# Two chained attentions on one Trainium2 core: the maxima of the softmax computed as one stream through both attentions

## The reference

```python
# layer 0, per image: group norm, then attention with relative positions, 6 heads of 16
attn = einsum('bqd,bkd->bqk', q * SCALE, k) + rel_h[..., None] + rel_w[..., None, :]
out0 = softmax(attn) @ v                       # 1024 queries x 1024 keys
x = x + out0 @ proj_w + proj_b
# layer 1, per image: layer norm, causal attention, 6 heads of 16
att = where(causal, (q @ k.T) * scale, -max)
t = t + (softmax(att) @ v) @ w_proj
# layer 1, feed-forward: 4 experts, top 2 by the gate, exact gelu
t = t + sum_e gate_e * (gelu(ln(t) @ w1_e + b1_e) @ w2_e + b2_e)
```

## The kernel before

| pair | `ahead` before |
|---|---|
| layer 1, p = 0 | 18: layer 1's own fills 6 to 23 (the first six stand ahead of the attention, `LEAD`) |
| layer 1, p = 1 | 32: own fills 24 to 47, then the first 8 of `lead` |
| layer 1, p = 2 | 24: `lead` 8 to 31 (`lead` is the maxima of pair 0 of the next image's layer 0) |
| layer 0, p = 0 | 32: `attn0` 0 to 31 |
| layer 0, p = 1 | 32: `attn0` 32 to 63 |
| layer 0, p = 2 | none |

## Time and profile before

### The profile page before, as it was taken

The page is one execution under the profiler, slowest core; times in us unless marked ns, Lnnn a source line. Parts: engine busy times, 40 slices in busy tenths (PEclk is TensorE's granted clock), DMA queues, the critical chain, the costliest instruction groups (busy, mean ns, idle before and its releaser), DMA issues.

```text
span 2026.6 us, 24544 instructions
## 1 busy us (share of the span) xinstructions
PE 1719.8 (85%) x8928; PEld 687.1 (34%) x8928; DVE 1217.0 (60%) x2498; ACT 1071.3 (53%) x1377; POOL 297.9 (15%) x191
## 2 busy tenths in 40 slices
PE   1578488998899988998899988999889989998858
PEld 0122232343333433344333433334333433234333
DVE  6743577546764577636775467646775466744631
ACT  1236435674556734665456745567445745565433
POOL 6103101401032000501023010321005010200000
PEclk7589679999999999999899999999999999999979
DMA  6645454445535346444335355353454454323000
GB/s 174 137 88 158 116 135 79 104 113 171 93 65 154 87 129 112 103 119 156 71 74 121 96 171 101 65 157 104 123 95 103 117 158 84 75 52 93 14 11 8
DMA packets 63742, 212.10 MB, mean 105 GB/s; under 512 B 17414, under 2 KB 19079, under 8 KB 51206
## 3 DMA queue, kind: packets, MB, share of 16 engines
q1 hardware_dynamic: 61702, 210.04, 42.0%
q10 hardware_dynamic: 1920, 0.49, 0.1%
HBM read 115.62 MB, written 81.79 MB: 97 GB/s over the span
## 4 chain that ended last, share of the span: by engine, by line
PE 60%; DVE 21%; ACT 7%; DMA 6%; issue 4%; SPq 2%; POOL 0%; ACTq 0%; DVEq 0%
PE psS L716 13%; DVE mx L1462 9%; PE psOM L768 9%; PE psT L746 7%; PE psT L889 5%; PE psOM L776 5%; PE psS L903 5%; PE psT L749 4%; DVE mrow L1564 3%; DVE qs L1591 2%; PE psT L666 2%; ACT probs L1143 1%; DVE x L1573 1%; DMA qs<-negr 1%; DMA qs<-scr_h 1%
## 5 line engine op out<-in xcount | busy, mean ns | idle before, releaser
L1143 ACT ACTIVATE probs<-psT 128x1024 f32<-128x1024 f32 (+7 forms) x768 | 621.4, 836 | 490.4 <-PE psT L746 240.3
L1462 DVE TENSOR_REDUCE mx<-psS 128x1 f32<-128x512 f32 (+3 forms) x1152 | 680.7, 640 | 292.2 <-PE psS L716 227.1
L746 PE MATMUL psT<-qs,ks 128*128 128x512 f32 x768 | 344.8, 522 | 38.3 <-DMA qs<-negr 17.6
L716 PE MATMUL psS<-ka,qa 128*128 128x512 bf16 x768 | 306.0, 407 | 45.2 <-DVE mx L1462 26.2
L768 PE MATMUL psOM<-probs,v 128*32 128x512 f32 x1536 | 225.5, 610 | 1.3
L716 PEld LDWEIGHTS psS<-ka,qa 128*128 128x128 bf16 x768 | 72.3, 98 | 345.4 <-DVE mx L1462 282.0
L749 PE MATMUL psT<-qr,kr 97*128 97x512 bf16 (+3 forms) x576 | 184.1, 348 | 4.6 <-DMA qr<-negb 3.7
L889 PE MATMUL psT<-xf,w1s 97*128 97x512 f32 x384 | 185.3, 616 | 1.8 <-DVE mrow L1564 1.8
L746 PEld LDWEIGHTS psT<-qs,ks 128*128 128x128 f32 x768 | 144.0, 200 | 116.7 <-ACT probs L1143 41.9
L903 PE MATMUL psS<-probs,w2s 128*96 128x512 f32 x384 | 181.5, 598 | 0.8 <-ACT att L1202 0.8
L1591 DVE TENSOR_TENSOR qs<-psOM,qs 32x768 fp32r<-32x768 f32 x128 | 121.8, 952 | 95.9 <-ACT qs L1177 93.9
(11 more groups left out here) (165 smaller groups left out, 1711.8 us busy)
## 6 DMA issues: line engine op xcount, KB each, us to landing
qs<-scr_w SPq DMA_DIRECT2D x48, 512.0 KB, 5.3
qs<-scr_q SPq DMA_DIRECT2D x48, 384.0 KB, 7.4
scr_q<-split SPq DMA_DIRECT2D x32, 384.0 KB, 4.1
scr_k<-split SPq DMA_DIRECT2D x32, 384.0 KB, 4.6
scr_w<-qs SPq DMA_DIRECT2D x8, 1536.0 KB, 12.4
scr_h<-qs SPq DMA_DIRECT2D x16, 768.0 KB, 14.7
qs<-scr_h SPq DMA_DIRECT2D x96, 128.0 KB, 5.1
qr<-scr_q SPq DMA_DIRECT2D x8, 1152.0 KB, 7.9
```

The lines of the kernel that those rows point to most:

```text
L716: last = mm(bank[:, 0:n], q[0:rows, h, t * P:(t + 1) * P], k[0:rows, h, kc * HALF:kc * HALF + n], start=True, stop=not diagonal)
L746: last = mm(o[:, a:b], ks[:, p % 2, hh, keys], qs[:, p % 2, kt // 2 % 2, hh, a:b], start=True, stop=True)
L1143: A(probs[:, n % 4, q0:T], psT[:, t_slot(ts, m), q0:T], ACT.Exp).then_inc(t_free, 1)
L1462: V.reduce_max(mx[layer][:, p % 2, (h % 2) * NT + t, kc:kc + 1], psS[:, s_bank(st, fill), 0:max_cols(layer, t, kc)], AX).then_inc(s_free, 1)
```

## The change

A function `stream(layer, p, lead, first)` now gives each pair two lists out of one sequence of fills (layer 1's own, `lead`, `attn0`): `ahead`, spread over steps 0 to 5 as before, and `tail`, of 8 fills in layer 0 and 6 in layer 1, which are the first fills of the pair behind the next. A tail's fills are issued one at a time in steps 6 and 7, in layer 0 at every call of `between`, in layer 1 at every second; what is left of it is issued after the pair's last values.

| pair | `ahead` now | `tail` now |
|---|---|---|
| layer 1, p = 0 | 18: own 6 to 23 | 6: own 24 to 29 |
| layer 1, p = 1 | 18: own 30 to 47 | 6: `lead` 0 to 5 (none for the last image) |
| layer 1, p = 2 | 26: `lead` 6 to 31 | 6: `attn0` 0 to 5 |
| layer 0, p = 0 | 26: `attn0` 6 to 31 (first image: 32, from 0) | 8: `attn0` 32 to 39 |
| layer 0, p = 1 | 24: `attn0` 40 to 63 | none |
| layer 0, p = 2 | none | none |

On VectorE `group_var` moves from 6 to 12 fills behind `group_stats`, and `group_norm` behind the last of layer 1's own fills and the `mrow` that follows it. The number of instructions of each kind on each engine stays the same.

```diff
-LEAD_EARLY = 8
+TAIL = {0: 8, 1: 6}
+
+
+def stream(layer, p, lead, first):
+
+    later = [("attn0", f) for f in range(2 * PER_PAIR[0])]
+    if layer:
+        own = [("attn1", f) for f in range(2 * PER_PAIR[1])]
+        later = own + [("lead", f) for f in range(len(MAX_STEPS["lead"]))] + later if lead else own
+    ends = [0, PER_PAIR[1], 2 * PER_PAIR[1], 2 * PER_PAIR[1] + len(MAX_STEPS["lead"])] if layer else [0, PER_PAIR[0], 2 * PER_PAIR[0], 2 * PER_PAIR[0]]
+    begin = ends[p] + TAIL[layer] if p else LEAD if layer else 0 if first else TAIL[1]
+    return later[begin:ends[p + 1]], later[ends[p + 1]:ends[p + 1] + TAIL[layer]]
...
+                    ahead, tail = stream(layer, p, next_lead(it), it is None)
+                    points, sent = [0], [0, 0]
+
+                    def issue(fills):
+
+                        for stage, fill in fills:
                             if stage == "lead" and fill == 0:
...
                             max_scores(it, stage, fill)
-                        sent[0] = until
+
+                    def between(kt):
+
+                        points[0] += 1
+                        until = min(len(ahead), len(ahead) * points[0] // (5 * (NT - 2)))
+                        issue(ahead[sent[0]:until])
+                        sent[0] = max(sent[0], until)
+                        if kt >= NT - 2 and sent[0] == len(ahead) and points[0] % (1 + layer) == 0:
+                            issue(tail[sent[1]:sent[1] + 1])
+                            sent[1] += 1
...
                     values(p, NT - 1)
+                    issue(tail[sent[1]:])
...
                     group_stats(it, "gn")
-                    maxima(it, "attn1", range(per, per + 6))
+                    maxima(it, "attn1", range(per, per + 12))
                     group_var(it, "gn")
-                    maxima(it, "attn1", range(per + 6, per + 22))
+                    maxima(it, "attn1", range(per + 12, 2 * per))
                     group_norm(it, "gn")
-                    maxima(it, "attn1", range(per + 22, 2 * per))
```

More of the change, by code:

```diff
@@ L753, in scores @@
                             last.then_inc(t_full, 1)
-                        between()
+                        between(kt)
                 def values(p, kt):
@@ L778, in values @@
                         last.then_inc(p_used, 1)
-                n = PER_PAIR[layer]
                 lead = layer == 1 and next_lead(it)
```

## The result

| | before | after |
|---|---|---|
| median of 4 runs each, us | 2025.75 (2021.58 to 2027.63) | 1997.38 (1991.79 to 2006.92) |
| ratio to before, 95% interval | | 0.9868 [0.9824, 0.9911] |
| profiled execution, us | 2028.4 | 2000.13 |

A forecast was written before the change was run, and what follows sets the result against it. VectorE, reducing through two banks, was taken to set steps 0 to 5 of the 32-fill pairs, 0.60 us per fill. The terms summed to -60.2 us from 2028.4, 1968.2, median near 1967; 8-in-10 range 1950 to 2002.

The forecast's parts named there:

- B: Layer 0, p = 0, 32 to 26 fills and a tail of 8: -8.4 us in 7 images, +1.8 in the first; -6.6.
- A: Layer 0, p = 1, 32 to 24 fills: -4.8 us a pair (ends 3.2 and 5.5), -38.4 in 8 images.
- the rule: A step with n fills lasts about (n - 1) x 0.60 + 1.29 us: 3.1, 3.7, 4.3 for 4, 5, 6.
- C: Layer 1, p = 0, a tail of 6 behind the statistics: +1.75 us in six images, +0.3 in the last two; +11.1.
- D: Layer 1, p = 1, 32 to 18 fills and a tail of 6: -5.2 us in six images, -38.9 in all.
- E: Layer 1, p = 2, 24 to 26 fills and a tail of 6: +1.8 us in seven images, +12.6 in all.
- TensorE doesn't set the steps: Rival claimed the opposite: four-fill steps no shorter than five-fill ones, gains vanish, tails cost +51 us, 2079; chance 0.06.
- The load for p = 2: Rival in layer 0's p = 1: the last load lands too late, ScalarE waits 1.6 us, 13 in all, 1980; chance 0.13.
- The clock at the ends of layer 1's pairs: Rival: new TensorE waits at two pair ends lower the clock, 12 to 20 us in all, 1984; chance 0.14.
- The opposite that it named: End of layer 1's p = 2: the tail fills the wait and lifts the clock, up to 1 us in seven images.
- What would show it: Signs expected in the profile after: the pair and step lengths, much less waiting of fills for VectorE in sum.
- three signs of being wrong: Layer 0 four-fill steps above 3.4 us, ScalarE waiting at its negation for a DMA in layer 0's p = 1, longer `mix`.

The follow-up runs named there:

- e1_join: Changed kernel with `mrow` made by a reduction over one SBUF operand instead of a two-operand maximum: 1976.6 us, 0.9735 of the kernel before.
- e8_pool: Changed kernel with the two-operand `mrow`, but GpSimd's last `den` multiplication waits until layer 0's p = 0 `mrow` is made: 1979.39 us, 0.9759 of before.
- e2_before_join: Kernel before the change, with `mrow` made by the one-operand reduction: 2030.16 us, 1.0009 of the kernel before.
- e9_meet: Kernel before, with GpSimd's last `den` multiplication delayed until the 31st reduction, so it begins just ahead of `mrow`: 2036.39 us, 1.004 of before.
- e10_meet_join: Kernel before, with GpSimd's last `den` multiplication delayed until the 31st reduction and `mrow` made by the one-operand reduction: 2028.72 us, 0.9998 of before.
- e7_step0: Changed kernel with one-operand `mrow` and four fills beside the projections in step 0 of layer 0's p = 1: 1976.55 us, 0.9742 of before.
- e5_stats: Changed kernel with one-operand `mrow` and `group_stats` six reductions earlier, among the steps of layer 1's p = 0: 1985.19 us, 0.978 of before.
- e3_no_tail0: Changed kernel without layer 0's tail (0 fills instead of 8), layer 1 as changed: 2001.47 us, 0.9857 of the kernel before.

## Why the prediction was right in direction and half in size

- **B, step 6: this failed.** "Step 6 ... now has five fills, 3.69: +0.95". It lasted 7.80 us. The working counted fills and nothing else; no term held what GpSimd does at that moment, and `mrow` was taken at the length that it had in every one of its 40 places before. The change moved it 3.5 us forward in the pair, and the order of instructions has no time between two engines, so the meeting could be seen only by laying GpSimd's rows over VectorE's and moving the one. Without the meeting B is -7.0 for a forecast of -6.6, but that agreement is luck: the steps before gave 2.24 by the fills (forecast 3.0) and 0.6 more by the low clock that before had there in five of seven images and after has not, step 6 cost 1.55 (4.27 us; forecast 0.95), and step 7 and the wait behind it gave 0.15 (3.82 us; forecast 4.82). That the meeting is the cause is shown by e1_join and e8_pool, which remove the meeting on either side, by e2_before_join, where the edit finds nothing to remove, and by e9_meet and e10_meet_join, which make it and remove it in the other kernel. It is worth 21 to 23 of the 32 us missed: seven waits of 2.1 us and six falls of the clock at some 1.4.
- **A: a term mis-sized.** "Each fill taken out of them is worth 0.60 us", times eight, -4.8 a pair; measured -2.9. Three things make up the difference. The steps with four fills last 3.19 us and not 3.10: five times 0.09, 0.45 us. The 3.10 was read in layer 1, whose score matmuls are not those of layer 0; that TensorE's 2.95 and VectorE's 3.1 fit badly, as the forecast's lower end has it, is likely, but no run shows it alone. The fill of step 0 was hidden beside the projections of the next queries and keys, where VectorE had 3.2 us idle: 0.14 instead of 0.60, 0.46 us. And the steps of before were shorter than the rule makes them: step 1 took 3.38 us (840.13 to 843.51) and not 3.69, and step 5, by issue six fills, 3.68 (855.18 to 858.86) and not 4.29, because its last fills run into step 6: 0.92 us that couldn't be saved. The rule was read from steps in the middle of a pair and applied to all of them, without laying it over the pair itself first; the result lies even below the forecast's lower end of 3.2. e7_step0 shows the second point from the other side.
- **C, D and E held**: +1.85 for +1.75 a pair, -6.1 for -5.2, +1.2 for +1.8. D's steps gave more (13.2 us from first exponential to step 6, forecast 14.2), and its end cost what was written (+2.2 for +2.1). The 14.2 were borrowed from p = 0, which begins with 2.8 us at the lower clock (0.50 from 739.08 to 741.92); p = 1 of after does not, which may be the whole difference. C's end is VectorE's statistics and six reductions, and e5_stats shows that it doesn't help to move the statistics into the steps.
- **The rivals.** TensorE doesn't set the steps: they shortened. The load for p = 2 was in time. It is issued 9.0 us before ScalarE negates, without an idle time; at the median of 7.4 us to landing 1.6 us are to spare, where 1.3 were forecast:

```profile
840.34 0.42 SPq L529 DMA_DIRECT2D qs<-scr_q  x1
```

```profile
849.31 0.25 ACT L1116 ACTIVATE negr<-psOM 32x128 fp32r<-32x128 f32 x1
```

- The clock at the ends of layer 1's pairs: the rival came in part. In the image of the rows the clock stayed up at the ends of p = 0 and p = 1:

```profile
745.00:752.00 7.00, 5.37 (x56) 2.51 (x49) 5.95 (x17) 1.77 (x6) 0.00 (x0) 1.00 0.13 30
```

```profile
764.00:771.00 7.00, 5.44 (x50) 2.28 (x43) 6.46 (x14) 1.74 (x6) 0.00 (x0) 1.00 0.42 68
```

But in the first image it fell at both ends, and in the sixth at that of p = 1:

```profile
287.77:291.17 3.40, 3.40 (x25) 1.45 (x23) 2.23 (x4) 0.55 (x2) 0.00 (x0) 0.50 0.51 125
308.25:311.65 3.40, 3.35 (x19) 1.15 (x20) 2.21 (x4) 0.54 (x2) 0.00 (x0) 0.50 0.54 130
1458.55:1461.95 3.40, 3.40 (x20) 1.19 (x19) 2.27 (x4) 0.39 (x2) 0.00 (x0) 0.50 0.20 41
```

That is three ends of twelve, each longer than the others of its kind by 1.4 to 1.5 us, 4.3 us in all; the rival wrote 12 to 20. The opposite that it named came too: in before the clock fell behind the end of p = 2 in five of seven images, in after in none, which gave back about 1 us each (an estimate: 0.6 in layer 0's first step and 0.4 ahead of it). The clock fell most often where nobody had looked, behind the wait for the held `mrow`: six times, some 1.4 us each.
- **What would show it.** "P = 1 of layer 1 at about 20" (19.1), "p = 2 at 23.7" (23.1) and an unchanged `mix` (0.8 us less in sum) came true. Layer 0's p = 1 at about 25 us to its last exponential's end (27.0), its "steps at 3.0 to 3.1" (3.19), the wait of fills "much less in sum" (hardly less) and "step 6 of layer 0's p = 0 at 3.7" (7.80) did not, and the last pointed at the cause at once. None of the three signs of being wrong came: they watched other places.

What stays open: in single profiled executions `mix`, which no kernel here touches, sums up to between 5 us less and 8 us more than before (e7_step0 and e3_no_tail0). Sums over a trace are uncertain by that much, and no more is made of them than the terms above.

## What to carry to other kernels

When an edit moves an instruction in time against another engine's, lay the two timelines over each other at the new place, and look for a VectorE instruction with two SBUF operands under a long GpSimd one; where the same value can be had from a reduction of one operand, that cost 0.03 us here and was never held up. Price such a stall by what is queued behind the instruction: the same 2.1 us cost 1.15 us with nothing behind it, 2.1 with the next pair's reductions there, and 3.5 where the clock fell as well. Look at more than one image before a term is called right: a stretch of low clock in one of the two pairs compared is worth 0.6 to 1.5 us here. Before a rule for the length of a step is used on fills that are taken out, lay it over all steps of the pair as they are: the first and the last ones here were not bound by it.

## What the runs showed of the hardware

- A VectorE `tensor_tensor` of two 128x32 SBUF operands, 0.19 us alone, took 2.32 us when it came 0.07 us behind a GpSimd multiplication of 2.35 us, and 1.92 when it came 0.48 us behind it: each time it ended with GpSimd's. An overlap with the last 0.1 us cost nothing; one with the last 0.3 us (a GpSimd instruction of 2.38 us in layer 0's p = 1 of after) made it 0.34 to 0.41. The reduction of one operand took 0.22 us in all 40 places, inside such a multiplication too.
- After a stretch of 3.0 us in which TensorE worked 0.62, the granted clock was at its lower level (0.51) for 3.4 us, in the middle of a stage in which it was otherwise at 1.00; so it was in six of seven images; in the other one (1505.00 to 1508.00), after the same 0.62 of 3.0 us, it stayed at 1.00. In e1_join, busy for 3.88 of the same 4.2 us, it stayed at 1.00 in all seven.
- Reductions of 512 columns from PSUM through two banks kept 0.60 us from start to start in a burst of four or five. In layer 0's steps with four fills, where TensorE's own work nearly fills the step, the burst of four took 2.58 instead of 2.49 us.
